# Windowed attention with global tokens, then top-1 experts: projections for pairs of windows in split halves, and expert group 1 prepared in steps 33 to 35

## What is computed

```
x = layernorm(x + attention(x))         # x is 2 x 2048 x 256, 16 heads of 16
x = layernorm(x + experts(x))           # 8 experts, 256 -> 64 -> 256, top 1
q, k, v = x @ wq.T + bq, x @ wk.T + bk, x @ wv.T + bv
scores = 0;  scores[own window of 128 tokens] = q k / 4
scores[every 32nd token, every 32nd token] += q k / 4     # 64 global tokens
attention = softmax(scores over all 2048) @ v @ wo.T + bo
expert = argmax(x @ Wg.T);  y = gelu((normalised(x) * s_e + b_e) @ W1_e + b1_e) @ W2_e + b2_e
```

## Time and profile before

| what | value |
|---|---|
| median of 3 runs | 474.56 us (470.91 to 475.12) |
| the profiled execution's own time | 476.29 us |
| its span | 474.8 us, mean granted clock 0.968 of full |
| PE, PE's weight loads busy | 91%, 77% of the span |
| DVE, ACT, POOL busy | 70%, 51%, 51% |
| scores of windows 1, 4, 5 begin | 44.40, 70.77, 80.35 us |

### The profile page before, as it was taken

One profiled execution on the slowest core, in us unless ns is written; L12 is line 12 of the kernel. 1 busy time (PEld: TensorE's weight loads), 2 busy tenths in 40 slices (PEclk: granted clock), 3 DMA queues, 4 the chain that ended last, 5 costly groups with the idle time before them and its releaser, 6 DMA issues.

```text
span 474.8 us, 15512 instructions
## 1 busy us (share of the span) xinstructions
PE 433.7 (91%) x6039; PEld 367.7 (77%) x6039; DVE 332.7 (70%) x822; ACT 243.0 (51%) x533; POOL 241.0 (51%) x329
## 2 busy tenths in 40 slices
PE   5869999999999999999999999898789998999981
PEld 4837888888888888888888888776557786877871
DVE  6882577765765766666657887553659888899776
ACT  2414465565565565565565564755544564544320
POOL 3342256456456456456465566443652675467441
PEclk9979999999999999999999999987989999999997
DMA  8830633000000000000000000100000011011112
GB/s 235 240 98 18 215 112 123 14 14 22 11 12 22 11 11 22 11 11 22 11 11 25 12 14 3 46 3 2 0 1 1 2 46 44 0 44 44 46 46 89
DMA packets 21962, 20.37 MB, mean 43 GB/s; under 512 B 3373, under 2 KB 21922, under 8 KB 21922
## 3 DMA queue, kind: packets, MB, share of 16 engines
q1 hardware_dynamic: 17684, 15.60, 10.6%
q10 hardware_dynamic: 4238, 4.22, 2.8%
HBM read 15.41 MB, written 4.41 MB: 42 GB/s over the span
## 4 chain that ended last, share of the span: by engine, by line
PE 77%; DVE 13%; issue 6%; ACT 1%; DMA 1%; ACTq 1%; DVEq 0%; POOL 0%; POOLq 0%
PE ps L1312 20%; PE ps L1343 10%; PE ps L1637 7%; PE ps L1352 7%; PE ps L1366 6%; PE ps L1472 6%; PE ps L1334 4%; PE ps L1372 4%; PE ps L1560 3%; PE ps L1357 2%; PE ps L1379 1%; DVE hm_part L1263 1%; DVE ysum L1254 1%; PE ps L1476 1%; DVE yvar L1234 1%
## 5 line engine op out<-in xcount | busy, mean ns | idle before, releaser
L1118 DVE TENSOR_REDUCE row_max_t<-ps 128x16 f32<-128x2048 f32 x31 | 71.0, 2291 | 58.0 <-PE ps L1343 57.8
L835 ACT ACTIVATE probs<-ps 128x1024 f32<-128x1024 f32 x64 | 62.2, 1022 | 29.1 <-PE ps L1357 29.1
L1312 PE MATMUL ps<-xT,wT 128*128 128x128 f32 x512 | 65.5, 281 | 0.0
L1312 PEld LDWEIGHTS ps<-xT,wT 128*128 128x128 f32 x512 | 59.6, 191 | 6.7 <-issue 6.6
L595 POOL TENSOR_TENSOR attn_t<-num_t,rden_t 128x256 f32<-128x256 f32 x32 | 19.9, 623 | 82.8 <-DVE rden_t L1145 82.8
L1637 PE MATMUL ps<-w_part,hm_part 128*128 128x256 f32 x384 | 55.3, 293 | 4.0 <-DVE hm_part L1263 3.5
L1472 PE MATMUL ps<-xh_parts,w_part 128*128 128x512 f32 x192 | 54.5, 420 | 2.3 <-issue 2.3
L1637 PEld LDWEIGHTS ps<-w_part,hm_part 128*128 128x128 f32 x384 | 48.8, 192 | 7.0 <-DVE hm_part L1263 4.3
L1343 PE MATMUL ps<-k_part,q_part 32*128 32x128 f32 x1584 | 51.5, 274 | 2.5 <-issue 1.1
L1343 PEld LDWEIGHTS ps<-k_part,q_part 32*128 32x128 f32 x1584 | 47.0, 186 | 8.5 <-issue 6.6
L558 POOL TENSOR_TENSOR q_part<-qf,q_part 128x512 fp32r<-128x512 f32 x32 | 41.5, 1298 | 21.8 <-ACT q_part L686 21.8
(11 more groups left out here) (214 smaller groups left out, 909.4 us busy)
## 6 DMA issues: line engine op xcount, KB each, us to landing
table<-rest_sums SPq DMA_DIRECT2D x4, 1088.0 KB, 5.8
xs<-in_L_attn_x_dram SPq DMA_DIRECT2D x32, 128.0 KB, 2.1
rows<-in_L_attn_x_dram ACTq DMA_DIRECT2D x4, 1024.0 KB, 8.0
out_dram<-yout SPq DMA_DIRECT2D x7, 512.0 KB, 2.8
w<-in_L_ffn_W_dram SPq DMA_DIRECT2D x2, 256.0 KB, 8.3
w<-in_L_ffn_W_dram SPq DMA_DIRECT2D x1, 512.0 KB, 3.9
out_dram<-yout SPq DMA_DIRECT2D x2, 256.0 KB, 2.1
w_raw<-in_L_attn_wq_dram SPq DMA_DIRECT2D x1, 256.0 KB, 2.8
```

The costliest lines, as they stand in the source:

```text
L835: act.activation(probs[:, 2 * h:2 * h + 2, :], ps[:, 2 * h:2 * h + 2, :], ACT.Exp).then_inc(probs_ready, 1)
L1118: dve.tensor_reduce(row_max[:], ps_all, op=ALU.max, axis=AX.X).then_inc(max_ready, 1)
L1312: last = mm(out, lhsT(c), rhs(c), start=(c == 0), stop=(c == KC - 1))
```

## The change

Windows are projected in pairs. In an even step t PE computes the queries and, further down, the keys of windows t+2 and t+3, and in an odd step the values of the pair t+1, t+2. Queries and keys are now split products too: 12 matmuls of 256 columns each for a pair (`turned_product`), with `wq_part` and `wk_part` made at the start; `xT` is gone. The keys come behind the bounds, the values of an odd step take the place of queries and keys, and x of the next pair (four transposes) is turned in odd steps ahead of the attention rows. ACT makes x's high part for a pair in one copy of 512 columns, DVE makes the low part (`low_of_x`) at the head of an even step, ahead of the row maximum, and the keys' low parts at the head of an odd step. POOL has no part in x any more. SP loads two windows at once. W2 is loaded in step 24 and split in steps 25 and 26. The sum for `b1` is a product with all experts' rows, masked on DVE (`own_bias`, end of step 31) and summed in four small matmuls in step 32. Group 1 is prepared in steps 33 to 35, and chunk 3 of group 0 is computed there.

```diff
-            def load_x(w, p):
-                need(sp, xT_in_psum, w - 1)
-                sp.dma_start(xs[:, p, :], x_w[:, bass.ds(w, 1), :]).then_inc(xs_ready[p], 16)
+            def load_x(w):
+                need(sp, xT_in_psum, w // 2)
+                sp.dma_start(xs[:], x_w[:, bass.ds(w, 2), :]).then_inc(xs_ready, 16)
...
-                if not steady and t == NW - AHEAD:
-                    sp.wait_ge(v_in_psum, NW)
-                    sp.wait_ge(x_low_ready, NW)
+                if not steady and t == FACTORS_AT:
+                    sp.wait_ge(rest_ready, NW // 2 + 1)
                     sp.dma_start(w2[:], w2_dram.rearrange("(c e) h d -> (e h) c d", e=EPC)).then_inc(ld_w2, 16)
...
-            def x_low(w, p):
-                pool.wait_ge(x_high_ready, w + 1)
-                pool.tensor_tensor(x_part[1][:], xT[:, p, :, :], x_part[0][:].bitcast(fp32), ALU.subtract).then_inc(x_low_ready, 1)
             def q_low(w, s):
-                pool.wait_ge(q_high_ready, w + 1)
-                pool.tensor_tensor(q_part[1][:, s], qf[:], q_part[0][:, s].bitcast(fp32), ALU.subtract).then_inc(q_ready, 1)
+                need(pool, turned_scores_in_psum, w - 3)
+                pool.wait_ge(q_high_ready, w // 2 + 1)
+                pool.tensor_tensor(q_part[1][:, s], qf[:, s % 2], q_part[0][:, s].bitcast(fp32), ALU.subtract).then_inc(q_ready, 1)
...
                 if ahead:
-                    need(pool, turned_scores_in_psum, t - 1)
                     q_low(t + AHEAD, (s + AHEAD) % SLOTS)
+                if not steady and t in (FACTORS_AT + 1, FACTORS_AT + 2):
+                    half = slice((t - FACTORS_AT - 1) * FC // 2, (t - FACTORS_AT) * FC // 2)
+                    pool.wait_ge(w2_high_ready, 1)
+                    pool.tensor_tensor(w2_part[1][:, half, :], w2[:, half, :], w2_part[0][:, half, :].bitcast(fp32),
+                                       ALU.subtract).then_inc(w2_low_ready, 1)
                 if not steady and t == NW - 1:
                     for pair in range(2):
                         take_low(0, 0, pair)
+                if not steady and t in (NW + 1, NW + 2):
+                    hidden_low(0, 0, t - NW - 1)
+                if not steady and t == NW + 2:
+                    for pair in range(2):
+                        take_low(1, 1, pair)
...
-            def turned_x(w, p):
-                act.wait_ge(xT_in_psum, w + 1)
-                need(act, v_in_psum, w)
-                copy(xT[:, p, :, :].rearrange("p c n -> p (c n)"), ps_xq[:, 0:HID]).then_inc(xT_ready, 1)
-                copy(x_part[0][:].rearrange("p c n -> p (c n)"), ps_xq[:, 0:HID]).then_inc(x_high_ready, 1)
+            def turned_x(w):
+                act.wait_ge(xT_in_psum, w // 2 + 1)
+                need(act, v_in_psum, w // 2)
+                copy(x_part[0][:].rearrange("p c w n -> p (c w n)"), ps_xq).then_inc(x_high_ready, 1)
...
             def keys_of(w, s):
-                need(act, turned_scores_in_psum, w - 3)
-                act.wait_ge(k_in_psum, w + 1)
-                key_high(s, ps_kv).then_inc(k_high_ready, 1)
+                need(act, turned_scores_in_psum, w - 2)
+                act.wait_ge(k_in_psum, w // 2 + 1)
...
-                if ahead:
-                    turned_x(t + AHEAD, p)
+                if ahead and p == 0:
+                    turned_x(t + AHEAD)
+                if cur and p == 0 and (steady or t > 0):
+                    values_of(t, s)
+                if live(t + 1, steady) and p:
+                    keys_of(t + 1, (s + 1) % SLOTS)
...
-                if not steady and t == NW + 2:
-                    act.wait_ge(turned_scores_in_psum, NW)
+                if not steady and t == FACTORS_AT + 1:
                     act.wait_ge(ld_w2, 16)
                     copy(w2_part[0][:], w2[:]).then_inc(w2_high_ready, 1)
+                if not steady and t == NW + 2:
+                    for pair in range(2):
+                        evacuate(1, 1, pair, False)
+                    hidden(0, 0, 2)
+                    keep_logits(1)
+                    hidden_high(0, 0, 2)
+                    for pair in range(2):
+                        scale_rows(2, pair)
+                if not steady and t == NW + 3:
+                    hidden(0, 0, 3)
+                    keep_onehot(1, 1)
+                    hidden_high(0, 0, 3)
...
+            def low_of_x(w):
+                dve.wait_ge(x_high_ready, w // 2 + 1)
+                dve.tensor_tensor(x_part[1][:].rearrange("p c w n -> p (c w n)"), ps_xq,
+                                  x_part[0][:].rearrange("p c w n -> p (c w n)").bitcast(fp32), ALU.subtract).then_inc(x_low_ready, 1)
+            def queries_of(w):
+                need(dve, q_ready, w)
+                dve.wait_ge(q_in_psum, w // 2 + 1)
+                for k in range(2):
+                    for c in range(KC):
+                        last = dve.scalar_tensor_tensor(qf[:, k, c, :, :],
+                                                        ps_xq[:, (2 * c + k) * P:(2 * c + k + 1) * P].unsqueeze(1).broadcast_to([P, 2, P]),
+                                                        bq_col[:, c:c + 1], q_scale[:], ALU.add, ALU.mult)
...
+                if ahead and p == 0:
+                    low_of_x(t + AHEAD)
+                if live(t + 1, steady) and p:
+                    keys_of(t + 1, (s + 1) % SLOTS)
...
+                    dve.wait_ge(b1_in_psum, 1)
+                    dve.scalar_tensor_tensor(own_bias, others_off[0:EXPERTS].rearrange("r c n -> r (c n)"), 0.0,
+                                             ps[0:EXPERTS, 5, :], ALU.is_equal, ALU.mult).then_inc(own_bias_ready, 1)
                 if not steady and t == NW:
...
+                    dve.wait_ge(b1_sums_in_psum, 1)
+                    dve.tensor_tensor(b1s[:], ps[:, 5, 0:FC], b1[:], ALU.add).then_inc(ffn_w_ready, 1)
+                if not steady and t == NW + 2:
+                    for pair in range(2):
+                        take_high(1, 1, pair)
+                if not steady and t == NW + 3:
+                    for k in range(ROUTE_STEPS):
+                        route(k, 1)
...
-            def turn_x(w, p):
-                need(pe, qf_ready, w)
-                pe.wait_ge(xs_ready[p], 16 * (w // 2 + 1))
+            def turn_x(w):
+                need(pe, qf_ready, w // 2)
+                pe.wait_ge(xs_ready, 16 * (w // 2 + 1))
                 for c in range(KC):
-                    last = nc.tensor.transpose(ps_xq[:, c * P:(c + 1) * P], xs[:, p, c * P:(c + 1) * P], ident[:])
+                    for k in range(2):
+                        last = nc.tensor.transpose(ps_xq[:, (2 * c + k) * P:(2 * c + k + 1) * P], xs[:, k, c * P:(c + 1) * P], ident[:])
...
+            def turned_product(bank, i):
+                terms = [(a, b, c) for a, b in SPLIT for c in range(KC)]
                 for o in range(KC):
-                    last = product(ps_xq[:, HID + o * P:HID + (o + 1) * P], lambda c: wT[:, WQ, c, o * P:(o + 1) * P],
-                                   lambda c: xT[:, p, c, :])
-                last.then_inc(q_in_psum, 1)
-            def keys_of(w, p):
-                need(pe, v_ready, w)
-                for o in range(KC):
-                    last = product(ps_kv[:, o * P:(o + 1) * P], lambda c: wT[:, WK, c, o * P:(o + 1) * P],
-                                   lambda c: xT[:, p, c, :])
-                last.then_inc(k_in_psum, 1)
+                    for j, (a, b, c) in enumerate(terms):
+                        last = mm(bank[:, o * 2 * P:(o + 1) * 2 * P], w_part[i][b][:, c, o * P:(o + 1) * P],
+                                  x_part[a][:, c, :, :].rearrange("p w n -> p (w n)"), start=(j == 0), stop=(j == len(terms) - 1))
+                return last
+            def queries_of(w):
+                pe.wait_ge(x_low_ready, w // 2 + 1)
+                if isinstance(w, int) and w == 0:
+                    pe.wait_ge(w_low_ready, 1)
+                turned_product(ps_xq, WQ).then_inc(q_in_psum, 1)
+            def keys_of(w):
+                need(pe, v_ready, w // 2)
+                if isinstance(w, int) and w == 0:
+                    pe.wait_ge(w_low_ready, 2)
+                turned_product(ps_kv, WK).then_inc(k_in_psum, 1)
             def values_of(w):
-                pe.wait_ge(k_ready, w + 1)
-                pe.wait_ge(x_low_ready, w + 1)
-                split_product(ps_kv[:, HID:2 * HID], x_part, wv_part).then_inc(v_in_psum, 1)
+                pe.wait_ge(k_ready, w // 2 + 1)
+                if isinstance(w, int) and w == 0:
+                    pe.wait_ge(w_low_ready, 3)
+                for k in range(2):
+                    last = split_product(ps_kv[:, k * HID:(k + 1) * HID], [part[:, :, k, :] for part in x_part], w_part[WV])
+                last.then_inc(v_in_psum, 1)
...
-                if ahead:
-                    queries_of(t + AHEAD, p)
-                    keys_of(t + AHEAD, p)
+                if ahead and p == 0:
```

(26 more changed lines are left out.)

234 lines of the change are left out of this document (102 added, 132 removed).

## The result

The changed kernel takes 456.99 us (median of 4 runs, 456.72 to 457.96), the kernel before 474.77 us beside it; the ratio is 0.965 (95% interval 0.960 to 0.970). Forecast were 469.0 us, 462 to 476. The direction was right, the gain of 17.8 us is three times the 5.5 forecast.

A forecast was written before the change was run, and what follows sets the result against it. PE's own work was taken to set the pace, with two chains of other engines close under it. Terms -4.5 + 0.2 + 2.0 + 0.5 + 0.7 - 4.4 = -5.5 from 474.56 gave 469.0 us, range 462 to 476.

The forecast's parts named there:

- the time that the sum was taken from: The median of the kernel before, 474.56 us, from which the summed gain of 5.5 was subtracted.
- my second rival: The low clock eats it: start loses 2.4, group 1 stretch gains only 2.5; 472.9 us, chance 0.25.
- Steady steps: Steps 6 to 23, nine pairs: 0.5 us less per pair, -4.5; over half of PE's saving becomes waiting for `attn`.
- Full queue of DVE: Late row maxima where work is appended on DVE: steps 2 to 5 +0.2, steps 24 to 29 +2.0 (0 to +3).
- step 26 would take over 10: Sign of the forecast: step 26 over 10 us, with a wait for the row maximum.
- the Newton operations: 27 DVE operations in steps 24 to 27, some 0.2 apart: add 0.5 in steps 24 and 26, 0.2 in 25 and 27.
- Start: Ahead of the steady steps: a new PE hole at 31 to 35 us may lower the clock; +0.5 (-1.5 to +2.4).
- Steps 31 and 32: DVE's mask and four small matmuls ahead of step 32's turned scores, b1 product 0.2 shorter; +0.7 (0 to +1.2).
- Group 1: Steps 33 to 35: rows and logits made early, `route` late next, first chunk at 343.7 instead of 348.14; -4.4.
- The waits don't come: DVE's extra work in steps 4, 26, 28 finds room, start gains 1.0, group 1 6.5; 460.8 us, chance 0.17.
- The slower rival: Pair-wide instructions hold the row maximum in even steps, making pairs longer; 483 us, or some 480; chance 0.08.

The follow-up runs named there:

- experiment 5: The kernel before with no edit, run again for a second trace; 469.5 us.
- experiment 1: The changed kernel with the sum for b1 put back to 16 fp32 products of 2 columns; 456.8 us.
- the 59 runs: Runs of the kernel before beside the experiments: 38 below 473 us, down to 468.8, and 21 from 473.6 to 475.4.
- experiment 6: The changed kernel with the four transposes of x behind the attention rows in odd steps; 463.5 us.
- experiment 10: The changed kernel with the last 3 of the 12 value products of an odd step moved behind the bounds; 456.6 us.
- experiment 7: The changed kernel with two more unused operations like x's low part ahead of the row maximum in even steps; 463.2 us.
- experiment 12: The changed kernel with old b1 sum, earlier group 1 logits, 3 late value products, stack_second_bias in steps 1 and 2, first-layer scaling halved behind steps 24 and 25; 454.3 us.
- experiment 13: Experiment 12 without its edit at the end: logits and chunk 3 of step 34 stand as in the changed kernel; 452.6 us.
- experiment 14: The changed kernel with 24 unused products of 256 columns in PE's hole ahead of the second pair's queries; 455.8 us.
- experiment 9: The changed kernel once more, unedited, on the chip of the next three experiments; 457.2 to 458.4 us, median 458.2.
- experiment 8: Experiment 4 with W2 loaded in step 30, its high part made in step 34, its low part by POOL behind step 35; 463.4 us.
- experiment 4: The changed kernel with the 2-column products for b1 and group 1 prepared behind step 35, both as before; 459.1 us.

## Why the prediction missed

Between the two profiled executions the kernel gained 19.5 us up to PE's end where 5.5 were forecast. The 14.0 us of miss are 5.0 in steps 31 and 32, 3.2 in steps 24 to 29, 1.5 each in the start, in steps 6 to 23 and in group 1, 0.9 in steps 1 to 5 and 0.4 behind. Two steps of the prediction failed: the time that the sum was taken from, and the terms for the steps in which DVE's queue is full.

**Against which time.** The sum was made against an execution with 17 us of half clock behind 314, and I treated that as part of the kernel. Beside experiment 5's trace, where step 31 begins to step 33's weigh ran at full clock, the change gives 12.6 us up to PE's end (458.1 to 445.4), not 19.5. The other 6.8 is half clock in that one execution of before: 4.7 in steps 31 and 32, 1.6 at the start, 0.6 in group 1. All traced executions of the changed kernel were without the 4.7; experiment 1 was without it too, so that the new form of the b1 sum took it away here isn't shown. The median beside the result is of this kind too: three of its four runs are 474.6 to 475.1, while the 59 runs have a median of 471.1, against which the gain is 14.1. The dips behind the 26th slice stood in the page, and my second rival used them, in the wrong direction only: that the change might lose more by the clock, never that it might stop losing. The 2-column products stood in the diff, and I costed their going at 0.2.

**Steady steps: right in mechanism, 1.3 us short.** Forecast even step 8.71, odd 8.26, measured 8.64 and 8.19; scores to attention rows 7.85 for 7.92. A part of PE's saving does turn into a wait for `attn`, as said, but 0.28 of 0.9 and not more than half (the prediction's own 0.55 kept of 0.9 would make it 0.35). Experiments 6 and 10 show the chain from both sides. The 0.5 per pair was rounded down from 0.55, and two steps each 0.07 too long make most of the rest: nine pairs gave 5.8 to 6.0, not 4.5. (Its sums at 5.37 in the even step should be 5.34, which changes nothing.)

**Full queue of DVE: the step that failed.** I put steps 2 to 5 at +0.2 and 24 to 29 at +2.0; they gave -0.4 and -1.2, 3.8 us between them. (Step 1, for which the sum had no term, gave 0.4 more: 9.15 became 8.78.) In steps 24 to 29 the sum had 3.5 us lost on DVE, and 0.7 were. DVE in the changed kernel, steps 4, 26 and 28 (scores at 68.95, 257.50 and 275.01):

```profile
71.61 0.67 DVE L971 TENSOR_TENSOR x_part<-ps,x_part 128x512 fp32r<-128x512 f32 x1
72.21 2.27 DVE L1136 TENSOR_REDUCE row_max_t<-ps 128x16 f32<-128x2048 f32 x1
```

```profile
257.31 1.96 DVE L1220 TENSOR_TENSOR xh<-w,vecT 128x512 f32<-128x512 f32 x2
259.31 0.69 DVE L971 TENSOR_TENSOR x_part<-ps,x_part 128x512 fp32r<-128x512 f32 x1
259.92 2.28 DVE L1136 TENSOR_REDUCE row_max_t<-ps 128x16 f32<-128x2048 f32 x1
...
274.73 1.57 DVE L1226 TENSOR_TENSOR w_part<-xh,w_part 128x1024 fp32r<-128x1024 f32 x1
...
276.82 2.27 DVE L1136 TENSOR_REDUCE row_max_t<-ps 128x16 f32<-128x2048 f32 x1
```

The mechanism is there in steps 4 and 26: the row maximum starts 3.26 and 2.42 behind the scores where 3.7 and 2.8 were forecast, and the steps take 10.23 and 9.30; that step 26 would take over 10 was a sign named ahead, and it failed. Four mis-sized terms took the rest. The appended work starts 0.2 to 0.4 ahead of the step, not with it. Most pieces overlap the next by 0.06 to 0.08, which a sum of lengths counts twice. So in step 28 the row maximum starts at 1.81, not 2.4, and costs nothing. The 0.45 that PE could spare I called gone, while a row maximum at 1.8 is still in time, though only just: in experiment 7 step 28 pays for all that is added. And the Newton operations (0.1 apart, not 0.2) held nothing up: step 24 took 8.65 where I had added 0.5. In experiments 12 and 13 the moved work brings back just these two steps' loss, which agrees.

**Start: the mechanism right, the sign open.** Forecast +0.5, -1.5 to +2.4; 43.4 against 42.85 in experiment 5's trace is +0.6, against the first trace -1.0. Four traces with before's start give 42.9 to 44.4, the changed kernel's two 43.4 and 44.0, so the forecast is neither confirmed nor refuted within its range. That the new hole brings the clock down was the reason, and experiment 14 shows it. The Trainium skill (TensorE: Matmul & The Clock Gate, HAM oscillation) has this rule, and the traces agree: half clock behind the hole in twelve, none in the three that fill it. The Trainium skill (TensorE: Matmul & The Clock Gate, What's actually happening) says that the number of slow matmuls at a kernel's start varies from run to run; here the half clock at the start of one kernel lasts 3.4 us in one trace and 6.8 in another (experiment 9).

**Steps 31 and 32: right, if at full clock.** Forecast +0.7; 17.01 against 16.59 in experiment 5's trace is +0.42, and 0.3 by the second trace.

**Group 1: near in size, wrong in its parts.** Forecast -4.4 for the first chunk; it came 18.0 behind step 33's weigh in both traces of before and 13.3 now, -4.7. (Up to the second layer it is -5.4 beside experiment 5, 20.75 to 15.39, as half clock lies behind the chunk there.) But I let all of it come from rows and logits made early. Up to the first chunk, experiment 8 against 4 gives 2.4 to W2's low part leaving POOL, and experiment 4 against 1 gives 2.4 to the early preparing (15.71 against 13.31): together the 4.7. POOL's low parts were a late item; what stood ahead of them on POOL was W2, and I left that row out. Before:

```profile
339.94 2.54 POOL L640 TENSOR_TENSOR w_part<-w,w_part 128x1024 fp32r<-128x1024 f32 x1
```

That the sum came near is luck: the half that I hadn't seen made up for the half that the early preparing didn't give. What is late next is `route` as said. PE, DVE and POOL of the changed kernel:

```profile
326.60 2.61 POOL L561 TENSOR_TENSOR xh_parts<-ffn_rows,xh_parts 128x512 fp32r<-128x512 f32 x2 [0.36 <-DVE xh_parts L1091]
...
328.37 0.89 DVE L1106 TENSOR_TENSOR hit<-hit,rank 128x32 f32<-128x32 f32 x1
...
329.95 0.39 PE L1468 MATMUL ps<-ident_b,onehot 128*24 128x128 bf16 x4 [2.49 <-DVE onehot L1111]
```

**The rivals.** "The waits don't come" (460.8) was the nearest in time, with the right places: DVE's work does find room in step 28 and mostly in 26. The slower rival, pair-wide work holding the row maximum, is refuted by experiment 7: it takes more than 1.1 us of further work on DVE in an even step before it begins to cost.

## What to carry to other kernels

Take two traces of the kernel before and compare their granted clock stretch by stretch ahead of any sum; here two traces of one kernel lie 6.8 us apart, nearly all of it in stretches with half clock. Where a sum goes over a queue in which work is appended, take the row's start from what releases the first piece, and step on by start-to-start distances, not lengths. When work leaves an engine, read what was queued behind it there: a split with no due time belongs where its engine has room, as W2's did.

## What the runs showed of the hardware

- With 16 products of 2 columns (1.95 us) in it, 21 of 59 executions of one kernel took over 473 us, and none of 22 with a product of 512 columns, a mask and four small products in their place. Two traces, the first of before and experiment 13's, show half clock right behind the 2-column products; in the first it cost 4.7 us up to step 33. Seven other traces of kernels with these products don't show it.
- 24 unused products of 256 columns in a hole of 3.3 us kept the clock at full speed in three traces of three; 16 transposes behind it took 1.91 instead of 3.56 us.
- A cast from SBUF to SBUF on DVE took 0.43 us alone, 1.21 beside POOL's 1.46, and 2.28 beside POOL's 2.53. The Trainium skill (SBUF — State Buffer, SBUF: two separate sides) says that the two engines' shared ports are held for a whole instruction; the trace agrees. Both long casts end 0.29 behind the end of the POOL operation that was running when they were issued (329.84 for 329.55, 328.73 for 328.44), and so do eight more in experiment 4's trace, 0.28 to 0.29 behind it, with lengths of 0.43 to 2.12; the three others issued beside POOL there ended later than that and took their 0.42.
